# A graph network with attention on one core: layer 2's linear attention moved into the block of its edge pass, with three smaller edits

## What is computed

```
xn = layernorm(x)
# graph part (8 heads of 32)
h = xn @ W + b;  e = leaky_relu(h_src[src] + h_trg[trg], 0.2);  p = exp(e - max)
gnn = segment_sum(h[src] * p, trg) / (segment_sum(p, trg) + 1e-10)
# mixing part: linear attention over all nodes
q = elu(xn @ Wq.T) + 1;  k, v = elu(xn @ Wk.T) + 1, xn @ Wv.T
mix = (q @ (k.T @ v)) / maximum(q . sum(k), 1e-6) @ Wproj.T + bproj
x = x + gnn + mix
```

## Time and profile before

| what | us |
|---|---|
| time, three runs | 6693.02, 6673.39, 6698.75; median 6693.02 |
| the profiled execution, its run time | 6705.66 |
| its span in the trace | 6703.8 |
| PE busy, mean granted clock | 4507.2 (67%), 0.779 |
| DVE, POOL, ACT busy | 3252.3 (49%), 2706.6 (40%), 1396.5 (21%) |
| layer 2's attention, in the trace | 3930 to 4194 |
| layer 2's edge pass: until the first sum, sums | 4194 to 4248, 4248 to 4882 |
| the last layer's pass | 5594 to 6328 |
| layer 1: edge_scores, weighted_sums | 2102 to 2946, 3021 to 3350 |

### The profile page before, as it was taken

One profiled execution on the slowest core, in us unless ns is written; L12 is line 12 of the kernel. 1 busy time (PEld: TensorE's weight loads), 2 busy tenths in 40 slices (PEclk: granted clock), 3 DMA queues, 4 the chain that ended last, 5 costly groups with the idle time before them and its releaser, 6 DMA issues. The chain is left out here.

```text
span 6703.8 us, 72009 instructions
## 1 busy us (share of the span) xinstructions
PE 4507.2 (67%) x18094; PEld 3156.5 (47%) x18094; DVE 3252.3 (49%) x7708; ACT 1396.5 (21%) x5100; POOL 2706.6 (40%) x2773
## 2 busy tenths in 40 slices
PE   0488845557776766647747665688849996777643
PEld 0256523335663433324446533566627774555543
DVE  6235444442016546657751245577752224587722
ACT  0122200003213444431142220000013332111111
POOL 2456656660112555527641210666600004566332
PEclk9988866668887665559968887566679998899866
DMA  4100023231114877756522210444410003222323
GB/s 146 51 2 2 2 81 92 90 89 63 45 45 151 250 229 234 231 143 206 159 75 81 76 40 0 114 113 113 102 40 0 0 0 95 75 85 85 78 91 107
DMA packets 407856, 616.84 MB, mean 92 GB/s; under 512 B 76553, under 2 KB 304285, under 8 KB 407108
## 3 DMA queue, kind: packets, MB, share of 16 engines
q0 software_dynamic: 124448, 324.61, 17.5%
q1 hardware_dynamic: 279908, 284.99, 13.3%
q10 hardware_dynamic: 3154, 3.20, 0.2%
HBM read 475.70 MB, written 137.50 MB: 91 GB/s over the span
## 5 line engine op out<-in xcount | busy, mean ns | idle before, releaser
L837 POOL DMA_INDIRECT m_rows<-support,far_at x440 | 422.1, 959 | 1033.8 <-POOLq L97 750.1
L3296 POOL DMA_INDIRECT g_sc_rows<-keyval,src_at x440 | 437.4, 994 | 495.0 <-ACT g_sc_rows L3280 178.6
L3921 POOL DMA_INDIRECT g_sp_rows<-h,src_at x440 | 444.8, 1011 | 468.3 <-POOLq L97 264.2
L847 PE MATMUL g_sums_bank<-g_sums_rows,g_sums_same 128*125 128x256 f32 x880 | 350.6, 536 | 297.9 <-issue 284.6
L493 POOL DMA_INDIRECT records<-record,place_at x416 | 420.6, 1011 | 282.2 <-issue 119.4
L837 POOL DMA_INDIRECT g_sums_rows<-h,far_at x440 | 416.6, 947 | 234.1 <-issue 115.6
L3969 PE MATMUL g_sp_bank<-g_sp_rows,g_sp_same 128*125 128x264 f32 x880 | 453.8, 616 | 56.4 <-issue 27.9
L3315 PE MATMUL g_sc_pair<-g1q_parts,g_sc_near 125*128 x1320 | 334.8, 385 | 141.8 <-DVE g_sc_rows L3362 84.4
L847 PEld LDWEIGHTS g_sums_bank<-g_sums_rows,g_sums_same 128*125 128x125 f32 x880 | 199.1, 256 | 449.3 <-issue 402.0
L3280 ACT ACTIVATE g_sc_rows<-g_sc_rows 128x64 f32<-128x64 f32 x1320 | 318.1, 242 | 416.2 <-DVE g_sc_rows L3362 309.3
L847 PE MATMUL m_half<-m_rows,m_same 128*125 128x256 f32 x880 | 278.4, 418 | 133.1 <-issue 123.1
(11 more groups left out here) (706 smaller groups left out, 9999.9 us busy)
## 6 DMA issues: line engine op xcount, KB each, us to landing
kept<-g_sc_rows SPq DMA_DIRECT2D x440, 128.0 KB
g_sp_rows<-kept SPq DMA_DIRECT2D x440, 128.0 KB
xnT<-sorted_rows SPq DMA_DIRECT2D x80, 256.0 KB
answer_rows<-f_answer SPq DMA_DIRECT2D x64, 256.0 KB
g_sc_local_in<-local_rows SPq DMA_DIRECT2D x55, 250.0 KB
g_sp_local_in<-local_rows SPq DMA_DIRECT2D x55, 250.0 KB
answer_rows<-zero SPq DMA_DIRECT2D x1, 9856.0 KB
sorted_rows<-zero SPq DMA_DIRECT2D x1, 8192.0 KB
```

The costliest lines, as they stand in the source:

```text
L837: nc.gpsimd.indirect_dma_start(self.rows[:, k, :], None, self.table, bass.IndirectOffsetOnAxis(ap=core.far_at[:, s:s + 1], axis=0)).then_i ...
L847: nc.tensor.matmul(self.halves[s % slots], self.same[:, s % self.RING, :], self.rows[:, s % self.SLOTS, :], start=True, stop=True).then_in ...
L3296: nc.gpsimd.indirect_dma_start(rows[:, k, :], None, table, bass.IndirectOffsetOnAxis(ap=core.src_at[:, s:s + 1], axis=0)).then_inc(gathere ...
L3921: nc.gpsimd.indirect_dma_start(self.rows[:, k, :], None, self.table, bass.IndirectOffsetOnAxis(ap=core.src_at[:, s:s + 1], axis=0)).then_i ...
```

## The change

**Layer 2.** The phase m2_att is gone, and `attended_sums` is now `attended_mix`, which runs the stages of `Mixing` in the block of the edge pass. A table gives 26 `kv` slots of some six steps each (159 steps in all), `context`, and then for each of 13 runs `read0`, `out`, `read1` and `q` with five to six steps each (281 steps). On PE, DVE and ACT the stage comes ahead of its slot's steps. To have banks for it, the sums have three instead of five, the expansions one instead of two, the keys and values one (which also takes half of the read-out), and the contexts two (which later take queries and outputs). The gathers have 32 slots instead of 40. The expansion for the group three ahead is done two at a time in the second half of a group. The clamp is passed as `guard`. The output rows of two tiles are added to x by one operation of 125 x 512. SP loads the mixing weights ahead of the first group's rows.

**The last layer.** `WeighedSums` takes the place of `Sums`: one grouped compare of 128 x 1000 in SBUF for eight steps, two groups ahead in three buffers (`marks`), ACT multiplies each step's one-hot by the weights (440 activations of 128 x 125, 12 steps ahead), and the bank that held the ramp becomes a third bank for the sums.

**Layer 1.** `pair_on_act` gives every other pair to ACT and every other to DVE (110 and 110, where it was 165 and 55). `weighted_sums` has a third `same` buffer and makes its compares two groups ahead.

The core of the diff (`linear_attention` is removed as a whole):

```diff
+class WeighedSums(Sums):
+    HELD = 3
+    LEAD = 12
...
+    def weigh(self, act, s):
+        if s % GROUP == 0:
+            act.wait_ge(self.matched, s // GROUP + 1)
+        nc.scalar.activation(self.mark(s), self.mark(s), ACT.Copy, scale=core.near_weight[:, s:s + 1]).then_inc(self.weighed, 1)
+
+    def match(self, v, g):
+        if g >= self.HELD:
+            v.wait_ge(self.summed, GROUP * (g - self.HELD + 1))
+        nc.vector.tensor_tensor(self.marks[:, g % self.HELD], bcast_mid(core.ramp[:, 0:P], shape),
+                                bcast_last(core.near_local[:, g * GROUP:(g + 1) * GROUP], shape), ALU.is_equal).then_inc(self.matched, 1)
...
+    def add(self, v, s):
+        if k == 2 and g + self.HELD - 1 < GROUPS:
+            self.match(v, g + self.HELD - 1)
...
@@ gnn3_mix3
-            halves, ramp = [ph.ps(f"half{k}") for k in range(2)], ph.ps("ramp")
+            halves = [ph.ps(f"half{k}") for k in range(3)]
...
+                for s in range(sums.LEAD):
+                    sums.weigh(act, s)
+                for (stage, r, _), steps in zip(slots, spans):
...
+                    for s in steps:
+                        if s + sums.LEAD < STEPS:
+                            sums.weigh(act, s + sums.LEAD)
@@ edge_scores
-        return pair % 4 != 3
+        return pair % 2 == 1
@@ weighted_sums
-        same = ph.sb("same", [W, 2, GROUP, P])
+        same = ph.sb("same", [W, 3, GROUP, P])
...
-                if s % GROUP == 1 and s // GROUP + 1 < GROUPS:
-                    compare(s // GROUP + 1)
+                if s % GROUP == 1 and s // GROUP + 2 < GROUPS:
+                    compare(s // GROUP + 2)
@@ Attend
-    SLOTS, BANKS = 40, 5
+    SLOTS, BANKS = 32, 3
...
-            if g >= 2:
-                pe.wait_ge(self.taken, g - 1)
+            if g:
+                pe.wait_ge(self.taken, g)
...
-        if s + 3 * GROUP < STEPS:
-            self.expand_pe(pe, s + 3 * GROUP)
+        if k >= 4 and g + 3 < GROUPS:
+            for there in (2 * k - 8, 2 * k - 7):
+                self.expand_pe(pe, (g + 3) * GROUP + there)
@@ attended_mix
+        mixing.place(ph, {"kv": [kv], "ctx": ctx, "q": qbank, "nd": [kv], "o": obank})
...
+        slots = [("kv", t, 26 if 0 < t < NT else 13) for t in range(NT + 1)] + [("context", 0, 0)]
+        behind = {"q": 0, "read1": 1, "read0": 1, "out": 2}
+        for i in range(len(RUNS) + 2):
+            for stage, work in (("read0", 26), ("out", 20), ("read1", 26), ("q", 20)):
...
+            pe.wait_ge(mixing.loaded, mixing.nload)
+            for (stage, r, _), steps in zip(slots, spans):
+                if stage == "kv":
+                    mixing.kv_pe(pe, r)
...
+                for s in steps:
+                    attend.step_pe(pe, s)
...
@@ gnn2_mix2
-        linear_attention(core, "m2_att", "L2_mix_Wq", [("L2_mix_Wkv", None)], "L2_mix_Wproj", core.x, clamp=1e-6)
-        attended_sums(core, attend, own, saved)
+        attended_mix(core, attend, own, saved)
```

## The result

| | kernel before | changed kernel |
|---|---|---|
| runs, us | 6693.0, 6673.4, 6698.8, 6686.7 | 6485.7, 6488.5, 6488.0, 6463.9 |
| median | 6689.9 | 6486.9 |
| span of the profiled execution | 6703.8 | 6484.0 |

The ratio is 0.9686, with a 95% interval of 0.9670 to 0.9702: 3.1% faster, 203 us by the medians and 220 by the two profiled spans. The prediction said 6465, 228 us less.

The account below looks back on a forecast made before the run. No engine was taken to bound the whole program, each stage being read alone; layer 2 -198 us, last layer -30, edge scores and weighted sums 0 summed to -228, from 6693 to 6465 us, range 6370 to 6580.

Parts of the forecast that it names:

- the nearest mixture: Layer 2's loop: PE's clock times busy share taken as 0.68 from the last layer's pass, for a loop of 690 us.

Follow-up runs that it names:

- e5: Kernel before with only class Attend as in the changed kernel (three sum banks, one expansion bank, 32 slots), layer 2's attention still separate; 6292.3 us, ratio 0.9999.
- e6: Kernel before with only layer 2's expansions moved, two at a time behind the sums of steps 4 to 7 of a group; 6292.6 us, ratio 1.0004.

## What to carry to other kernels

Before taking work from an engine, look whether it stands in time in which the engine waits for itself: a compare of 0.34 to 0.40 us between two dependent adds was free, and as an operation of 1.19 us for eight, with the products on another engine, it cost some 30 us. Where two engines hand a stream to each other and each has stages of 2 to 3 us of its own, the depth of the banks between them decides: a third bank gave 50 us in one loop and a fourth 17 in another, and moving a stage past its wait without it gave nothing. A loop in which another engine sets the pace, as POOL did in e5 and e6, tells nothing about the banks' depth. Merging a chain-bound phase into a loop with room is worth the phase less the work that the busiest engine gets; to price the loop, add up each engine's work and take clock times busy share from the nearest mixture, not the old loop's, but as a check only: here it ran from 0.67 to 0.72 for the same work on PE.

## What the runs showed of the hardware

The chips differed by 6% on the same kernel: medians of 6690, 6659, 6290 and 6283 us for the kernel before. The difference shows in the stages that gather: edge_scores took 834.2 us at 232 GB/s on the first chip and 704.7 at 275 on the third, while weighted_sums took 325.6 and 325.7. In the new loop the kv section took 247 to 253 us on the first two chips and 219 to 225 on the others, the read-out section, with three banks and its reciprocals, 434 to 447 and 437 to 440. Why the transfers move more there is not known from these runs.

TensorE's granted clock in layer 2's loop without mixing was 0.63 and 0.67 on two chips; on the third it was 0.75 in e6, which differs in the expansions' place alone, where 0.67 is estimated for the kernel before. With the mixing stages in it it was 0.82 to 0.85 on all four. Before, PE was busy 94% of the 40 us from 4320 at a clock of 0.50, which is 1.2 GHz; a window of the same length early in the new loop, with PE less busy, shows a mixture nearer to 2.4 GHz:

```profile
4120.00:4160.00 40.00, 32.59 (x122) 22.48 (x121) 27.81 (x70) 4.48 (x15) 26.99 (x26) 0.83 0.40 106
```
